# A two-pass mixture-of-experts and attention kernel: expert numbers loaded sooner, shared products deferred, first attention steps reordered

## The reference

```python
x = x + 0.5 * ffn(layernorm(x))
x = x + attention(layernorm(x))
x = x + 0.5 * ffn(layernorm(x))

def ffn(x):                      # 2048 tokens
    shared_out = swiglu(x, shared_gate, shared_up, shared_down)     # 128 -> 256 -> 128
    logits = x @ gate_w.T        # 8 experts
    top_id, score = argmax(logits), sigmoid(max(logits))
    # each token goes to its one expert, with x * score as the expert's input
    return shared_out + swiglu(x * score, r_gate[top_id], r_up[top_id], r_down[top_id])

def attention(x):                # per batch, 16 heads of 8 features, rotary q and k
    return softmax(q @ k.T / sqrt(8)) @ v @ W_o.T
```

## Time and profile before

| | |
|---|---|
| median of 3 runs | 333.96 us (333.08 to 336.78) |
| the profiled execution, its own time | 334.64 us |
| its span, first to last instruction | 332.8 us |
| mean granted TensorE clock | 0.949 of full speed |
| PE busy | 295.1 us (89%) |
| DVE busy | 230.0 us (69%) |
| ACT busy | 204.3 us (61%) |
| POOL busy | 152.3 us (46%) |

### The profile page before, as it was taken

How to read it: one execution, slowest core, us unless ns; L and a number is a source line. 1 busy time by engine, 2 the same in 40 slices (tenths; PEclk the granted TensorE clock), 3 DMA queues, 4 the chain that set the end, 5 groups by cost and what they waited for, 6 DMA issues and landing times.

```text
span 332.8 us, 6641 instructions
## 1 busy us (share of the span) xinstructions
PE 295.1 (89%) x2162; PEld 183.1 (55%) x2162; DVE 230.0 (69%) x639; ACT 204.3 (61%) x449; POOL 152.3 (46%) x281
## 2 busy tenths in 40 slices
PE   6799979999577899989999999989999896999960
PEld 2665656666333455645656555555574555566640
DVE  7974523356688798988888898979946782443332
ACT  8235225554662699998989898997658240444420
POOL 7346704668444343444353544340302673265560
PEclk9959999999985899999999999999999999899995
DMA  6961172120030000000000000000000115310135
GB/s 208 349 272 48 48 189 36 42 73 33 39 97 0 2 1 1 2 3 2 1 2 2 1 2 0 3 2 0 2 3 9 42 48 130 95 39 39 41 118 190
DMA packets 18768, 18.41 MB, mean 55 GB/s; under 512 B 5072, under 2 KB 16208, under 8 KB 18352
## 3 DMA queue, kind: packets, MB, share of 16 engines
q1 hardware_dynamic: 16240, 12.87, 12.6%
q0 software_dynamic: 2496, 5.13, 4.3%
HBM read 10.29 MB, written 7.71 MB: 54 GB/s over the span
## 4 chain that ended last, share of the span: by engine, by line
PE 40%; DVE 27%; issue 11%; POOL 10%; ACT 6%; DMA 4%; POOLq 0%; SPq 0%; ACTq 0%; DVEq 0%
PE bank L1083 31%; DVE negmax L876 12%; POOL y_by_token L347 5%; PE bank L1276 4%; DVE xn L667 3%; DVE qT L869 3%; ACT kT L576 2%; ACT probs L569 2%; POOL xs_sorted L338 2%; PE bank L1221 1%; DVE stats L677 1%; DVE rs L893 1%; DVE rc L891 1%; DMA x<-in_x 1%; PE bank L1157 1%
## 5 line engine op out<-in xcount | busy, mean ns | idle before, releaser
L876 DVE TENSOR_REDUCE negmax<-bank 128x2 f32<-128x512 f32 x128 | 83.4, 681 | 8.2 <-PE bank L1083 7.6
L569 ACT ACTIVATE probs<-bank 128x512 f32<-128x512 f32 x128 | 71.0, 602 | 14.4 <-PE bank L1083 13.7
L347 POOL DMA_INDIRECT y_by_token<-ys,xg x46 | 44.9, 976 | 47.1 <-issue 24.6
L1083 PE MATMUL bank<-kT,qT 128*128 128x512 bf16 x128 | 50.1, 395 | 3.3 <-DVE negmax L876 2.3
L1083 PE MATMUL bank<-qT,kT 128*128 128x256 bf16 x256 | 49.9, 278 | 0.5 <-ACT qT L587 0.3
L840 DVE TENSOR_TENSOR rh<-rsg,bank 128x256 f32<-128x256 f32 x46 | 19.3, 419 | 42.9 <-ACT rsg L545 42.9
L1083 PE MATMUL bank<-rgu,xgT 128*128 x92 | 48.2, 607 | 0.3 <-ACT xgT L537 0.3
L338 POOL DMA_INDIRECT xs_sorted<-xs,slot x32 | 32.3, 1008 | 31.8 <-ACT xs L497 17.4
L545 ACT ACTIVATE rsg<-bank 128x256 f32<-128x256 f32 x46 | 17.6, 383 | 44.1 <-PE bank L1083 44.1
L1276 PE MATMUL bank<-tabb,parts 128*128 128x128 bf16 x384 | 31.3, 229 | 6.6 <-POOL parts L378 3.2
L1276 PEld LDWEIGHTS bank<-tabb,parts 128*128 128x128 bf16 x384 | 26.0, 103 | 14.7 <-POOL parts L378 5.8
(11 more groups left out here) (122 smaller groups left out, 498.6 us busy)
## 6 DMA issues: line engine op xcount, KB each, us to landing
rgu<-in_rgu SPq DMA_DIRECT2D x1, 2048.0 KB, 11.3
xg<-xs_sorted SPq DMA_DIRECT2D x6, 258.0 KB, 4.3
xs_sorted<-xg SPq DMA_DIRECT2D x1, 1483.5 KB, 6.1
xg<-xs_sorted SPq DMA_DIRECT2D x6, 193.5 KB, 3.4
x<-in_x SPq DMA_DIRECT2D x4, 256.0 KB, 4.1
rdn<-in_rdn SPq DMA_DIRECT2D x1, 1024.0 KB, 13.4
xs<-y_by_token SPq DMA_DIRECT2D x8, 128.0 KB, 3.0
xs<-y_by_token SPq DMA_DIRECT2D x4, 256.0 KB, 3.8
```

What stands on the lines that cost most here:

```text
L347: g.indirect_dma_start(y_dram, bass.IndirectOffsetOnAxis(ap=xg[:, j, D:ROW].bitcast(U32), axis=0), ys[:, j, :], None, bounds_check=N + SLO ...
L569: a.activation(probs[:, h % 8, :], stbank[st_bank(i, h)][:], ACT.Exp, scale=float(DH) ** -0.5).then_inc(exp_done, 1)
L876: v_.tensor_reduce(negmax[:, w, t, h0 + 2 * pair:h0 + 2 * pair + 2], sbank[k % 2][:].rearrange("p (a s) -> p a s", a=2), AX.X, ALU.max, ne ...
L1083: return t_.matmul(o_, l, r, start=start, stop=stop, **k)
```

## The change

The change has these parts.

1. **Clock filler.** `idle_products` puts products of zeros, 512 columns each, that nothing reads, at new places: 3, 3, 1 and 2 among the turns and logits of `ffn(0)`; 4 after the key turn and 8 after the eighth `scores` of step -1.
2. **Expert numbers.** `find_experts` moves ahead of `shared_add(1)`. In PE's program the wait for them and the loads into registers move ahead of `turn_g(0)` and of `shared_down` of chunks 2 and 3, in both layers.
3. **Deferred shared products.** `shared_down` gets two PSUM banks. In layer 1 its chunks 2 and 3 move out of the way: two tiles of chunk 2 into round 22 of the routed loop, one into round 23, the last one and chunk 3 behind the loop; their `shared_add` move between the pieces of `add_experts` at the end.
4. **Scatter order.** `BEFORE_RSTD` goes from 3 to 4: one more tile is written on POOL before the last chunk's standard deviation of layer 1.
5. **First attention steps.** The projections of batch 1 move ahead of qa, into banks 4 and 5 of `stbank`; in step -2 `copy_turned` moves ahead of the remainders; `rope(0)` goes ahead of the copies of queries and keys. The split of batch 0's first maxima moves from POOL to DVE (`split_first`), ma is turned at n = 11 (was 13) and copied by DVE (was ACT), and `scores_t` of heads 0 and 1 of batch 0 run in places 12 and 13 of step -1 (was step 0). `add_experts(0, 2)` and `moments_of(3)` move from n = 11 to 14; normalising batch 2 moves from the end of step -1 to n = 1 of step 0, its turn and copy from n = 0 to 2.

```diff
-BEFORE_RSTD = 3
+BEFORE_RSTD = 4
...
-        gate_bank, up_bank, down_bank, rank_bank = bank[4:6], bank[6:8], bank[1], bank[2]
+        gate_bank, up_bank, down_bank, rank_bank = bank[4:6], bank[6:8], (bank[1], bank[0]), bank[2]
...
                 shared_hidden(2)
                 if n:
                     place_rows(n, 1)
+                find_experts(n)
                 shared_add(1)
-                find_experts(n)
                 shared_hidden(3)
-                shared_add(2)
-                shared_add(3)
+                if n == 0:
+                    shared_add(2)
+                    shared_add(3)
...
                     for k in range(len(PIECES)):
+                        if PIECES[k][0] in (8, 12):
+                            shared_add(PIECES[k][0] // CHUNK)
                         add_experts(n, k)
...
                 if i == -2:
+                    copy_turned()
                     remainder(0)
                     remainder(1)
                     third(0)
                     third(1)
-                    copy_turned()
                     return
+                def split_first():
+
+                    dve.wait_ge(s_reduced, HH)
+                    m = negmax[:, 0, :, 0:HH]
+                    mc = [parts[0][:, :, 0, 0:HH, MCOL + k] for k in range(3)]
+                    st.link(v_.tensor_copy(mc[0], m))
+                    st.link(v_.tensor_tensor(mrem[:], m, mc[0], ALU.subtract))
+                    st.link(v_.tensor_copy(mc[1], mrem[:]))
+                    v_.tensor_tensor(mc[2], mrem[:], mc[1], ALU.subtract).then_inc(m_split, 1)
+
...
                 if i == -1:
+                    rope(0)
                     copy_queries("qa")
                     copy_keys()
-                    rope(0)
                     rope(1)
...
                     if i == -1 and n == 11:
+                        split_first()
+                        copy_queries("qb")
+                        copy_queries("ma")
+                    if i == -1 and n == 14:
                         add_experts(0, 2)
                         moments_of(3, v)
-                    if i == 0 and n == 0:
+                    if i == 0 and n == 2:
                         turn(Turn(-1), "turned")
...
+                    if i == 0 and n == 1:
+                        turn(Turn(-1), "normalise")
+                        moments_of(3, v)
...
+            def idle_products(count, b=0, to=bank[6]):
+
+                zeros = kT[b][:, 0, :, :].rearrange("p a s -> p (a s)")
+                for k in range(count):
+                    mm(to[:], zeros[:, 0:P], zeros)
+
...
                     turn_chunk(n, 0)
+                    idle_products(3)
                     logits(n, 0)
                     turn_chunk(n, 1)
+                    idle_products(3)
                     logits(n, 1)
                     count(n, 0)
+                    idle_products(1)
                     turn_chunk(n, 2)
+                    idle_products(2)
                     turn_chunk(n, 3)
                     logits(n, 2)
                     logits(n, 3)
...
                 shared_gate(n, 3)
                 shared_up(n, 3)
-                shared_down(n, 2)
+                pe.wait_ge(expert_ready, n + 1)
+                pe.load(expert_regs, expert[0:1, :])
+                experts = [t_.snap(r_, min_val=0, max_val=E - 1) for r_ in expert_regs]
                 if n:
 
                     pe.wait_ge(ssilu, 2 * CHUNKS * (n + 1))
                     turn_g(0)
                     turn_g(1)
-                pe.wait_ge(expert_ready, n + 1)
-                pe.load(expert_regs, expert[0:1, :])
-                experts = [t_.snap(r_, min_val=0, max_val=E - 1) for r_ in expert_regs]
-                shared_down(n, 3)
+                else:
+                    shared_down(n, 2)
+                    shared_down(n, 3)
...
+                        if n and j == SLOT_TILES - 1:
+                            shared_down(n, 2, range(0, 2))
...
+                    if n and j == SLOT_TILES:
+                        shared_down(n, 2, range(2, 3))
...
+                if i == -1:
+                    project(0)
+                    project(1)
                 for n in range(H):
-                    if T.e:
+                    if T.e and not (i == 0 and n < 2):
                         scores_t(n)
...
-                    if i == 0 and n == 0:
+                    if i == 0 and n == 2:
                         attention_turn(Turn(-1), "rows")
...
+                    if i == -1 and n == 1:
+                        idle_products(4, 1, pvbank)
+                    if i == -1 and n == 11:
+                        idle_products(8, 1, pvbank)
+                    if i == -1 and n in (12, 13):
+                        attention_turn(Turn(0), n - 12)
...
-                    if n == (13 if i == -1 else 14) and T.m:
+                    if n == (11 if i == -1 else 14) and T.m:
                         pe.wait_ge(m_split, 2 * (i + 1) + 1)
                         turn_parts("ma")
...
             ffn(1)
+            shared_down(1, 2, range(3, CHUNK))
+            shared_down(1, 3)
```

More of the change, by code:

```diff
@@ L637, in attention_turn @@
                         second(1)
-                    if n == (10 if i == -1 else 13) and T.m:
+                    if n == 13 and T.m and i >= 0:
                         copy_queries("ma")
@@ L885, in rope @@
                         dve.wait_ge(rotated, 2 * (i + 1) + t + 1)
-                    bk = work[uses.index(name) % 2]
+                    bk = stbank[t] if i == -1 else work[uses.index(name) % 2]
                     qk = bk[:, 0:2 * D]
@@ L942, in copy_turned @@
                     dve.wait_ge(filled["xT"], i + 4)
-                    v_.tensor_copy(xnT2[:, v, :], work[uses.index("xT") % 2][:, 0:L]).then_inc(emptied["xT"], 1)
+                    bk = pvbank if i == -1 else work[uses.index("xT") % 2]
+                    v_.tensor_copy(xnT2[:, v, :], bk[:, 0:L]).then_inc(emptied["xT"], 1)
                 if piece == "rows":
@@ L1044, in turn @@
                         v_.tensor_copy(oT[:], work[uses.index("oT") % 2][:, 0:L]).then_inc(emptied["oT"], 1)
-                    if n == (15 if i == -1 else 10) and T.nx:
+                    if n == 10 and T.nx and i >= 0:
                         normalise_batch()
@@ L1135, in shared_up, with shared_down @@
                     mm(up_bank[k][:], shgu[:, F + k * P:F + (k + 1) * P], xnT[:, c * 512:(c + 1) * 512]).then_inc(su_filled, 1)
[L1137 removed]
+            def shared_down(n, c, tiles=range(CHUNK)):
                 k0 = n * CHUNKS + c
[L1139 to L1142 removed]
+                if tiles[0] == 0:
+                    pe.wait_ge(sh_ready, k0 + 1)
+                    if c >= 2:
+                        pe.wait_ge(sy_added, k0 - 1)
+                for i in tiles:
                     for k in range(2):
[L1144 removed]
+                        ins = mm(down_bank[c % 2][:, i * P:(i + 1) * P], sh[:, c % 2, k, i * P:(i + 1) * P], shdn[:, k, :],
                                  start=(k == 0), stop=(k == 1))
[L1146 removed]
+                if tiles[-1] == CHUNK - 1:
+                    ins.then_inc(sy_filled, 1)
             def ffn(n):
@@ L1396, in attention_turn @@
                         turn_parts("ka")
-                    if n == (1 if i == -1 else 3) and T.pr:
+                    if i == -1 and n == 1:
[4 more added lines that the diff above has]
+                        attention_turn(Turn(0), n - 12)
+                    if n == 3 and T.pr and i >= 0:
                         project(0)
@@ L1429, in _ @@
             pe.wait_ge(keys_cleared, 1)
-            idle = kT[0][:, 0, :, :].rearrange("p a s -> p (a s)")
-            for k in range(IDLE_PRODUCTS):
-                mm(bank[7][:], idle[:, 0:P], idle)
+            idle_products(IDLE_PRODUCTS)
             ffn(0)
```

48 lines of the change are left out of this document (29 added, 19 removed).

## The result

The changed kernel took 329.37 us (median of 3 runs, 328.08 to 330.36) against 333.96 before: a ratio of 0.9877, with an interval of 0.9828 to 0.9926. Ratios in this text are taken from the fast runs alone, so they can differ a little from the quotient of two medians. The profiled execution took 330.36 us with a span of 328.5, 4.3 less than the 332.8 of before. The forecast had 6.5 less, and its range of 324.8 to 331.2 holds the result. So the direction and the mechanisms stood, and a third of the gain did not come. The rest of this text finds that third.

What follows compares the result with a forecast made beforehand. No single engine bounds the kernel (PE 40% of the chain, DVE 27%). Layer 0 0 + attention 2.4 + layer 1 4.1 = 6.5 us off 334.64 gives 328.1, or 327.5 against the median; range 324.8 to 331.2.

Steps and rivals of the forecast that it cites:

- Filler and logits in layer 0: Layer 0 routing: filler keeps full clock in the logits, second step's choice 0.95 us sooner; bounds 0 to 1.0.
- A new pause in layer 0: Ahead of layer 0's routed loop: PE pauses some 2.6 us, the clock falls, costing 1.0 us and eating the 0.95.
- Start of attention: First attention steps: first maximum 2.1 us sooner, first exponential near 102.3; 2.4 us won, bounds -0.5 to 3.2.
- Rival (3): Attention: DVE's added 1.5 us are not absorbed, so attention gives 0; 4.1 us won, 329.9 us; chance 0.12.
- The split: Start of attention: four small DVE operations splitting the first maxima, 0.7 to 1.0 us in all, taken as 0.9.
- The attention filler: Start of attention: 8 products of 0.21 lie beside the split; up to 1 us goes if the clock still falls.
- Layer 1: Loads ahead of the first turn, shared products deferred: 5.5 - 1.0 half clock - 0.4 tail = 4.1 us; bounds 1.3 to 5.1.
- the sequencer: Layer 1: the skill's rule would let shared_down run during register loads; the prediction followed the trace's 2.68 us pause instead.
- Rival (2): Layer 1: the pause is not the register loads and stays before the first gate product; 3.7 us won, 330.3; chance 0.11.
- rival (1): Both routed loops: no new clock falls, 2.0 us more; 8.5 us won, 325.5 us; chance 0.22.
- rival (4): Both routed loops: the clock, once low, stays low, losing 5.1 us each; 1.75 us slower, 335.7 us; chance 0.05.
- The tail: End of layer 1: two tiles of shared_down ahead of a late turn delay the last results and POOL's last write by 0.4 us.

Runs made afterwards that it cites:

- e1: The kernel before with parts 2, 3 and 4 alone, no filler and the old attention steps; 337.64 us, ratio 0.9863.
- e5: The changed kernel itself run again, as the standard for its group; 328.76 us, ratio 0.9888.
- e7: The changed kernel with layer 1's shared_down of chunk 2 back ahead of the register loads, chunk 3 alone deferred; 326.40 us, ratio 0.9791.
- e9: The changed kernel with layer 1's shared_down of chunks 2 and 3 both ahead of the register loads, only the adds deferred; 333.74 us, ratio 0.9738.
- e10: The changed kernel with BEFORE_RSTD back at 3, so part 4 alone undone; 335.50 us, ratio 0.9793.
- e8: The changed kernel with 13 more filler products in step 0 of attention; 328.76 us, ratio 0.9885.
- e12: The kernel of e7 without the 9 filler products of layer 0 and the 12 of attention; 336.24 us, ratio 0.9822.
- e2: The changed kernel without the filler of layer 0 and of attention; 336.51 us, ratio 0.9841.
- e4: The changed kernel with part 5 alone undone: old first attention steps, without their filler; 335.51 us, ratio 0.9801.
- e3: The changed kernel with ten and fourteen more filler products in the pauses ahead of the routed loops of layers 0 and 1; 334.82 us, ratio 0.9804.
- e6: The changed kernel with layer 1's register loads behind the first two turns, as before, the deferral kept; 328.73 us, ratio 0.9887.
- e11: The kernel of e7 run again in another group, 6 runs; 330.98 us, ratio 0.9664.

## Why the prediction was right, and where its sizes were off

**Filler and logits in layer 0: right.** Forecast 0.95 at the second choice. In the profiled run 0.45, because everything up to there ran 0.49 later than before (the slots of 18.50 at 18.99). The filler is not to blame: e1, without it, has the slots at 19.01. In e5, e7, e9 and e10 the choice stood at 18.43 to 18.57, 0.95 to 1.09 sooner than 19.52. The limit was, as said, DVE itself.

**A new pause in layer 0: right in kind, its price too low.** In the profiled run the clock fell behind a pause of 1.60 us where I had 2.6 and the pauses of before had been 2.68 and 2.80. That it falls there is luck in part: in e5, the same kernel, an earlier fall took the pause away. The step that failed is the price, "I take 1.0, between 0 and 1.7". I had read it from the loop of layer 1 before, 4.93 against 3.99 us. But there the slow stretch had begun 2.4 us earlier, under `shared_down`, so that only its rest fell into the loop. With the whole of it in the loop it is 5.58 - 3.99 = 1.59, in both loops. Twice 0.6 is 1.2 of the 2.2 us that are missing; most of the rest is the fall in step 0 (0.8), then 0.2 in steady attention.

**Start of attention: right to the first exponential, with a fall too many behind it.** From the turns to the first maximum I had 3.1 us; it is 3.17 (94.46 - 91.29). In e5 to e8, without a fall, place 4 comes 25.28 us after the last down product, 2.4 sooner than the 27.70 of before: the forecast exactly, though on another chip. In the profiled run the fall at 110 took 0.8 of it. Rival (3), that attention gives nothing, falls. Its worry was not idle, though: from the first exponential to place 4 it takes 10.30 us in e5 at full clock against 8.87 before, so DVE's added work shows there, as the forecast had allowed by giving place 4 less than the exponential. The split was mis-sized: its four operations took 1.38 us (99.36 to 100.74), where I had 0.9.

**The attention filler: the mis-sized term that the result hid.** I priced it at nothing, with "up to 1 us" if the clock fell in spite of it. The fall it prevents costs more: 2.36 us up to place 4 in e12, 0.62 of it by the first exponential, and 1.3 in e2. Without filler the reordered start takes 6.80 + 20.84 = 27.64 us in e12, which is what the old order took (27.70), and 26.57 in e2, where the old order took 27.57 (e1) and 27.20 (e4). So a good part of what part 5 brings hangs on its filler: a third of it by e2 and e3 (0.5 of 1.5 us against e1), all of it by e12's trace.

**Layer 1: right in sum, the half clock apart.** The first gate product follows 0.74 us after the turn, as forecast. I had the turn at 277.3, 0.2 behind its old place; it came 0.41 later after the slots, since only 0.74 us of the loads lay beside `shared_up` and the loads took 3.09 us. On the sequencer: in the kernel before, products that need no register stood still behind the loads, and e6 shows the pause going where the loads go. By the Trainium skill, Advanced Engine Details and Errata, section Sequencer Loop, other engine instructions can be read and queued while a control instruction executes; what e7 and e9 show is that products handed over *ahead* of the loads go on beside them, while nothing *behind* them starts. Rival (2), which took that rule to cover both sides, falls; rival (1), no falls, came true for the first loop in e5 to e8 and for the second in e3, e7, e8, e9 and e11; rival (4) never: no fall in a routed loop outlasted the fourth gate product.

**The tail: right in sign.** 0.19 us for the two tiles, where I had 0.4 (36.65 for 36.46 us from the fourth gate product to POOL's last write), and nothing behind it (8.73 us for 8.80).

**Two slips in the prediction's arithmetic.** Rival (2) gives 2.4 + 2.8 - 1.0 - 0.4 = 3.8 us won, not 3.7. And the upper end of the range, 331.2, does not follow from its terms: rival (2) with attention at its lower bound would be 333. Neither touches the forecast.

**What stays open.** Which pause brings a fall in a given run can't be told from these traces. Ahead of the second loop's first gate product pauses of 0.60, 0.95, 1.93 and 2.34 us brought none (e7, e9, e11, e8), while 2.35, 2.38 and everything from 2.65 to 4.43 did; ahead of the first, 1.60 us brought one in the changed kernel. Open too is where the difference of the chips comes from, below.

## What to carry to other kernels

In this kernel 23 register loads on PE stopped everything behind them for 3.0 us, 0.13 us each on average. Put independent products right ahead of them, as in e7, which beat the changed kernel in its group by 2.3 us: that hides the loads and fills the pause that would cost clock. When work is taken out from in front of a critical stretch, ask what PE does in the gap: here pauses of 1.60 and 2.35 us gave back 1.6 us per loop, beside 4.3 us won in all. A fall is cheap where little waits for the slow work, as behind the logits in e5, and dear at the entry of a loop. And when an edit comes with filler, price the fall that the filler prevents, over the whole stretch at half clock, and not the filler's own time.

## What the runs showed of the hardware that I had not expected

The clock's falls are not a fixed property of the program: the changed kernel fell in step 0 in one trace and not in the next (19.29 and 18.49 us from the first maximum to place 4), with the same instructions and the same pauses, and the second loop fell behind 2.38 us in e5 and not behind 2.34 in e8. One fall can also decide over another: the one from 19 us in e5 took away the pause ahead of the first loop (4.21 us for 5.58). A comparison of single traces can be off by 0.8 us for step 0 and 1.6 us for a loop's entry.

The chips differ by 3%, and part of it is visible. On the two chips where the kernel before took 342 us, some instructions that wait on another engine start late by microseconds with the releaser "remote", in all eight traces of those chips and in none of the other six. In layer 1 of e9 the DVE step that waited 0.29 us in the changed kernel stands for 3.12 us. First the changed kernel, then e9:

```profile
267.43 0.29 DVE L735 TENSOR_TENSOR over<-bank,tab 128x128 f32<-128x128 f32 x1 [0.29 <-PE bank L1108]
```

```profile
42.69 1.08 ACT L509 ACTIVATE sgate<-bank 128x512 f32<-128x512 f32 x2 [7.62 <-remote]
...
270.43 0.29 DVE L735 TENSOR_TENSOR over<-bank,tab 128x128 f32<-128x128 f32 x1 [3.12 <-remote]
```

The ACT row, ahead of the first routed loop, is why the first turn comes 7.2 us after POOL's last write in e9 instead of 4.6 to 4.9 in e5 to e8: DVE's hidden product needs it, the last 16 shared products wait 1.32 us for that (at 45.14), and the turn follows them. What holds these instructions was not found.
